# Routing in an attention and mixture-of-experts block: five operations fewer on VectorE, one addition on GpSimd, one more ranks matmul

## The reference

```
x = x + tanh(g_xattn) * xattn(layernorm(x), ctx)       # 16 query heads, 4 key heads, head size 128, rope
x = x + tanh(g_ffn)   * ffn(layernorm(x))
# ffn, for every token
probs = softmax(x @ w_router)                          # 8 experts
top_v, top_i = top_k(probs, 2); top_v = top_v / sum(top_v)
routed = sum over the 2 chosen experts of top_v * down(silu(x @ gate) * (x @ up)) * 2.5
ffn = routed + shared expert
```

## Time and profile before

| | |
|---|---|
| median of three runs | 1221.59 us (1221.35 to 1222.02) |
| the profiled execution: its own time, its span | 1223.99 us, 1222.2 us |
| busy: PE, DVE, ACT, POOL | 1199.6, 1037.9, 903.5, 941.1 us |
| granted TensorE clock, mean | 0.998 |

### The profile page before, as it was taken

The page is one execution under the profiler, slowest core; times in us unless marked ns, Lnnn a source line. Parts: engine busy times, 40 slices in busy tenths (PEclk is TensorE's granted clock), DMA queues, the critical chain, the costliest instruction groups (busy, mean ns, idle before and its releaser), DMA issues.

```text
span 1222.2 us, 31455 instructions
## 1 busy us (share of the span) xinstructions
PE 1199.6 (98%) x8765; PEld 1113.0 (91%) x8766; DVE 1037.9 (85%) x3014; ACT 903.5 (74%) x3774; POOL 941.1 (77%) x1124
## 2 busy tenths in 40 slices
PE   6899999999999999999999999999999999999999
PEld 3788999999999999999999999999999999999887
DVE  8788999999999999999989999988888777777554
ACT  7978787887888778887888877877777646666422
POOL 2778888888888888888888888888888525555585
PEclk9999999999999999999999999999999999999999
DMA  6634233332222222223333333332235636555485
GB/s 178 201 105 127 83 99 104 111 97 90 90 90 90 90 92 93 90 95 94 96 96 114 107 101 99 105 102 80 75 108 151 225 105 192 158 164 159 149 274 183
DMA packets 141079, 148.55 MB, mean 122 GB/s; under 512 B 13824, under 2 KB 124672, under 8 KB 140256
## 3 DMA queue, kind: packets, MB, share of 16 engines
q1 hardware_dynamic: 126096, 125.97, 34.2%
q0 software_dynamic: 6480, 17.77, 4.0%
q10 hardware_dynamic: 8448, 4.20, 1.2%
HBM read 66.93 MB, written 80.76 MB: 121 GB/s over the span
## 4 chain that ended last, share of the span: by engine, by line
PE 92%; DVE 4%; ACT 3%; issue 1%; DMA 0%; SPq 0%; DVEq 0%; ACTq 0%
PE b_kv L1801 14%; PE b_q L1787 14%; PE b_o L1885 13%; PE b_sc L1859 9%; PE b_aT L1874 9%; PE b_pT L1867 5%; PE b_qT L1848 4%; PE b_q L2121 3%; PE b_kv L2121 3%; PE b_kT L1844 2%; PE b_kT L2181 1%; PE b_o L2181 1%; PE b_kv L2181 1%; PE b_q L2181 1%; PE b_aT L2138 1%; PE b_pT L2138 1%
## 5 line engine op out<-in xcount | busy, mean ns | idle before, releaser
L1801 PE MATMUL b_kv<-w_group,kv_in_hi 128*128 128x256 f32 x992 | 204.9, 304 | 0.0
L979 ACT ACTIVATE probs<-b_sc,neg_max 128x128 f32<-128x128 f32 x512 | 180.6, 371 | 2.6 <-DVE neg_max L1343 2.1
L773 POOL TENSOR_TENSOR q_rot<-q_rot,q_sin 128x512 f32<-128x512 f32 x128 | 176.7, 1381 | 7.2 <-DVE q_sin L1333 2.4
L769 POOL TENSOR_TENSOR qk_r<-qk_me,minus_half 128x6 f32<-128x6 f32 x128 | 172.0, 1344 | 10.1
L1801 PEld LDWEIGHTS b_kv<-w_group,kv_in_hi 128*128 128x128 f32 x992 | 161.3, 190 | 7.3 <-issue 0.4
L1787 PE MATMUL b_q<-w_group,kv_in_hi 128*128 128x512 f32 x496 | 164.8, 413 | 0.4 <-DVE q_sin L1333 0.4
L1885 PE MATMUL b_o<-wo_hi,aT_hi 128*128 128x256 f32 x480 | 143.5, 299 | 0.3 <-DVE aT_lo L1357 0.3
L1859 PE MATMUL b_sc<-kT,qT 128*128 128x128 f32 x1024 | 136.3, 276 | 6.2 <-ACT qT L968 4.5
L776 POOL TENSOR_TENSOR q_rot<-q_rot,qk_r 128x512 f32<-128x512 f32 x128 | 133.7, 1044 | 10.0
L1801 PE MATMUL b_kv<-w_group,kv_in_lo 128*128 128x256 f32 x496 | 139.6, 282 | 0.0
L962 ACT ACTIVATE junk<-b_q 128x128 bf16<-128x128 f32 x512 | 134.0, 283 | 0.0
(11 more groups left out here) (332 smaller groups left out, 3977.3 us busy)
## 6 DMA issues: line engine op xcount, KB each, us to landing
xs_scratch<-zeros SPq DMA_DIRECT2D x34, 1032.0 KB, 6.2
s_in<-xs_scratch SPq DMA_DIRECT2D x71, 129.0 KB
yT_scratch<-yT SPq DMA_DIRECT2D x32, 256.0 KB
routed<-ys_scratch SPq DMA_DIRECT2D x32, 256.0 KB, 4.3
w_hi_all<-w_scratch SPq DMA_DIRECT2D x3, 1536.0 KB, 14.4
x_in<-in_x SPq DMA_DIRECT2D x32, 128.0 KB, 2.3
ctx_raw<-in_ctxT SPq DMA_DIRECT2D x32, 128.0 KB, 2.5
trig_scratch<-sincos SPq DMA_DIRECT2D x8, 512.0 KB, 5.9
```

What stands on the lines that cost most here:

```text
L769: nc.gpsimd.tensor_tensor(qk_r[g % 2][:], qk_me[:], minus_half[:, 0:REP + NB], ALU.pow).then_inc(r_ready, 1)
L773: nc.gpsimd.tensor_tensor(q_rot[g % 2][:], q_rot[g % 2][:], q_sin[g % 2][:], ALU.add) \
L979: last = nc.scalar.activation(probs[:, j, :], b_sc[:, j * P:(j + 1) * P], ACT.Exp, bias=neg_max[g % 2][:, j:j + 1], accum_out=row_sum[g % ...
L1801: last = nc.tensor.matmul(b_kv[:, s * 2 * HD:(s + 1) * 2 * HD], kv_in[p][a][:, c, 2 * s:2 * s + 2, :], wkv_of(b, c)[:, g % KVH, :], start= ...
```

## The change

For each tile DVE loses five operations: the two that made the shares from tanh (L1418, L1419), one of two comparisons (both are now one operation over 16 columns), the addition to `seen` and the operation that put expert x STRIDE to the rank. The gate and the constant 2.5 / 2 are multiplied into two small constants once, so y_share is one operation from tanh. The addition to `seen` goes to GpSimd for all tiles but the last two. The expert's first row comes out of PE: a constant tensor `starts` holds STRIDE / 128 x expert, and a third matmul with the matrix of ones adds it 128 times. `lead_tanh` moves from the end of g = 3 to g = 0, behind the squares of keys.

```diff
@@ gpsimd, in a unit
+                    if g == 0 and not first:
+                        need(pool, rk_done, t - 1)
+                        nc.gpsimd.tensor_tensor(seen[:], seen[:], mask[:], ALU.add).then_inc(seen_ready, 1)
@@ scalar, in a unit
+                    if g == 0 and not first:
+                        lead_tanh(t - 2)
                     if not (first and u == 0):
                         queries_out(n, g)
...
-                    if g == 3 and not (end or first and p == 0):
-                        lead_tanh(t - 1)
@@ vector: weights_and_mask
-                nc.vector.tensor_copy(top_f[:], top_i[:, 0:TOPK])
+                nc.vector.tensor_copy(top_f[:], top_i[:, 0:TOPK]).then_inc(pick_ready, 1)
+                need(dve, pick_ready, 2 * t + 1)
+                each = [P, TOPK, E]
+                nc.vector.tensor_tensor(pick[:], expert_no[:].unsqueeze(1).to_broadcast(each),
+                                        top_f[:].unsqueeze(2).to_broadcast(each), ALU.is_equal).then_inc(pick_ready, 1)
                 need(dve, lead_done, t + 1)
-                nc.vector.tensor_scalar(share[:, 0:1], lead_t[:], ROUTED_SCALE / 2, ROUTED_SCALE / 2, ALU.mult, ALU.add)
-                nc.vector.tensor_scalar(share[:, 1:2], lead_t[:], -ROUTED_SCALE / 2, ROUTED_SCALE / 2, ALU.mult,
-                                        ALU.add).then_inc(share_ready, 1)
-                need(dve, share_ready, t + 1)
-                for n in range(TOPK):
-                    last = nc.vector.tensor_scalar(pick[:, n, :], expert_no[:], top_f[:, n:n + 1], None, ALU.is_equal)
-                last.then_inc(pick_ready, 1)
-                nc.vector.tensor_scalar(y_share[p], share[:], gates[:, 1:2], None, ALU.mult)
-                need(dve, pick_ready, t + 1)
+                need(dve, wsin_ready, 8)
+                nc.vector.scalar_tensor_tensor(out=y_share[p], in0=gate_signed[:], scalar=lead_t[:], in1=gate_half[:],
+                                               op0=ALU.mult, op1=ALU.add)
+                need(dve, pick_ready, 2 * t + 2)
+                need(dve, seen_ready, t + 1)
                 nc.vector.tensor_tensor(mask[:], pick[:, 0, :], pick[:, 1, :], ALU.add).then_inc(mask_ready, 1)
@@ vector: rows_of_tokens, read_ranks
-                nc.vector.tensor_reduce(rank[:], ranked[:], AX.X, ALU.add).then_inc(rank_step, 1)
-                need(dve, rank_step, 2 * t + 1)
-                nc.vector.scalar_tensor_tensor(out=row_f[:], in0=top_f[:], scalar=float(STRIDE), in1=rank[:], op0=ALU.mult,
-                                               op1=ALU.add).then_inc(rank_step, 1)
-                need(dve, rank_step, 2 * t + 2)
+                nc.vector.tensor_reduce(row_f[:], ranked[:], AX.X, ALU.add).then_inc(rank_step, 1)
+                need(dve, rank_step, t + 1)
                 nc.vector.tensor_copy(row_i[p][:], row_f[:]).then_inc(row_ready, 1)
...
-                nc.vector.tensor_tensor(seen[:], seen[:], mask[:], ALU.add) \
-                  .then_inc(seen_ready, 1)
+                if isinstance(t, int) and t >= TILES - 2:
+                    nc.vector.tensor_tensor(seen[:], seen[:], mask[:], ALU.add).then_inc(seen_ready, 1)
@@ vector: first pair, u = 4 and u = 5
+                        nc.vector.tensor_scalar(starts[:], expert_no[:], float(STRIDE // P), None, ALU.mult)
...
+                            for to, m, sign in ((gate_signed, 0, 1), (gate_signed, 1, -1), (gate_half, 0, 1), (gate_half, 1, 1)):
+                                nc.vector.tensor_scalar(to[:, m:m + 1], gates[:, 1:2], sign * ROUTED_SCALE / 2, None,
+                                                        ALU.mult).then_inc(wsin_ready, 1)
@@ tensor: ranks
                 nc.tensor.matmul(b_kT[:, D:D + E], below[:], mask[:], start=True, stop=False)
+                nc.tensor.matmul(b_kT[:, D:D + E], ones[:], starts[:], start=False, stop=False)
                 last = nc.tensor.matmul(b_kT[:, D:D + E], ones[:], seen[:], start=False, stop=True)
```

More of the change, by code:

```diff
@@ L249, in flamingo @@
         lead, lead_t = few[:, 0:1], few[:, 1:2]
-        top_f, share, rank, row_f = [few[:, o:o + TOPK] for o in (4, 6, 8, 10)]
+        top_f, gate_signed, gate_half, row_f = [few[:, o:o + TOPK] for o in (4, 6, 8, 10)]
         pick = sb("pick", [P, TOPK, E], F32, late_at)
@@ L263, in flamingo @@
         assert x_res_at[0] <= x_res_end
-        late_at[0] += 128
+        starts = sb("starts", [P, E], BF16, late_at)
+        assert STRIDE % P == 0 and (E - 1) * (STRIDE // P) <= 256
+        late_at[0] += 64
         G_WIDE, D_WIDE = DC * GU // G_TILES, DN * D // D_TILES
@@ L369, in flamingo @@
         (wr_split, y_coarse, y_fine, below_ready, stats2, var2, ve2_done, rstd2_ready, y_normed, yT_done, yT_hi,
-         yT_lo, lg_done, lg_copied, top_found, lead_ready, lead_done, share_ready, pick_ready,
+         yT_lo, lg_done, lg_copied, top_found, lead_ready, lead_done, pick_ready,
          mask_ready, rk_done, rk_read, seen_ready, rank_step, row_ready) = map(sem, (
@@ L373, in flamingo @@
              "y_normed", "yT_done", "yT_hi", "yT_lo", "lg_done", "lg_copied", "top_found", "lead_ready",
-             "lead_done", "share_ready", "pick_ready", "mask_ready", "rk_done", "rk_read",
+             "lead_done", "pick_ready", "mask_ready", "rk_done", "rk_read",
              "seen_ready", "rank_step", "row_ready"))
```

## The result

The changed kernel takes 1224.16 us (median of 20 runs, 1223.55 to 1225.23), the kernel before in the same comparison 1222.05 (20 runs, 1221.35 to 1223.24): ratio 1.0018, 95% interval 1.0012 to 1.0024, 2.1 us slower. Forecast were 1219.2 and a range up to 1221.8. The profiled execution has a span of 1221.9 us at a granted clock of 0.998.

A forecast was written before the change was run, and what follows sets the result against it. PE was taken as the bound, with 92% of the chain. The terms -2.2 - 0.5 - 0.8 + 0.35 + 0.8 = -2.35 took the median 1221.59 to 1219.2 us, range 1217.8 to 1221.8.

The forecast's parts named there:

- What bounds the kernel: PE is 92% of the chain; its lateness, read from distances between starts, is 2.8 us over 27 tiles.
- the choice of the median: The forecast was taken from the runs' median, 1221.59 us, 2.4 below the profiled execution's 1223.99.
- Tanh, -2.2: Moving lead_tanh behind the squares of keys ends the late units g = 0, mostly behind the loop's jump: 2.2 us gained.
- the first rival: Another wait of the unit, or the jump itself, takes the gain, so the 2.2 stays: 1221.4 us, chance 0.17.
- Second pair, -0.5: Around 128 us the squares of keys no longer stand behind the waiting tanh on the chain: 0.5 us gained once.
- Five operations, -0.8: Less DVE work shortens PE's waits in g = 1 (0.4), at 105 us (0.2) and for the slot table (0.2).
- Constants, +0.35: Five small DVE operations making constants in the first pair, 0.07 each, all on the path: 0.35 us lost.
- Third matmul, +0.8: The added ranks matmul stands where PE is not idle: 32 x 0.026 = 0.8 us lost.
- So I take nothing: In g = 0, GpSimd's 1.33 us reciprocal root was taken not to delay DVE's two-input operations: no cost.
- Both are covered: The addition to seen on GpSimd, 0.2 to 0.3 or at most 0.7, fits in 1.07 us to spare before PE.
- The second rival: GpSimd's root (L769) shuts out DVE's y_share and mask in 14 units behind a jump: 9 us, 1228, chance 0.06.

The follow-up runs named there:

- R + C: Kernel before with routing off DVE, addition to seen on GpSimd, third matmul, and cosine table moved to g = 3; tanh not moved: 1222.27 us against 1222.21.
- T + R + C: The changed kernel with GpSimd's cosine table made one unit earlier, in g = 3: 1218.91 us against 1221.96 for the kernel before.
- T: Kernel before with only lead_tanh moved behind the squares of keys of g = 0: 1221.94 us against 1221.96.
- R: The changed kernel with tanh back at the end of ScalarE's g = 3: 1222.59 us against 1222.49 for the kernel before.
- C: Kernel before with only GpSimd's cosine table moved from g = 0 to g = 3: 1221.75 us against 1222.11.

## Why the prediction was wrong

- **What bounds the kernel**: right. PE's distances showed every effect. The profiled execution of before lay 2.4 over its median; its part behind unit 124 took 281.1, and in all twelve other traces 278.9 to 279.6. So the excess was there, and the choice of the median was right.
- **Tanh, -2.2**: right as a mechanism, and in size once nothing else is as late (R + C has a long stage of 784.95, T + R + C of 782.59). Timeline of ACT, kernel after, behind the jump; the squares of keys start 0.27 after heads_T (389.86), not 0.84, tanh with no idle time ahead of queries_out:

```profile
390.13 0.30 ACT L955 ACTIVATE junk<-b_kv 128x128 bf16<-128x128 f32 x1
...
390.63 0.24 ACT L1042 ACTIVATE few<-few 128x1 f32<-128x1 f32 x1
390.72 0.64 ACT L973 ACTIVATE qT<-b_qT 128x512 f32<-128x512 f32 x1
```

  But PE gets it only if nothing else is as late, and the same units had a second lateness behind the first (T alone: 0.0). I listed that as the first rival with 0.17, in g = 0; it sits in g = 1.
- **Second pair, -0.5**: the amount is right (126.20 to 133.96 is 7.76, before 8.27), but tanh alone gives 0.20 of it (T: 8.07); it takes R as well. And 0.45 of it is given back in the two late units behind it.
- **Five operations, -0.8**: PE's wait for the slot table went from 0.36 to 0.16, as forecast, the one for x_n at 105 us from 0.33 to 0.25 (0.2 forecast); the table's place was the rest of it (C takes it away). Mis-sized where it matters: that these operations also start GpSimd's sums earlier was not in the sum at all. With T and C in place R, third matmul included, is worth 1.7 us in the long stage (784.31 against 782.59) and 2.8 by the medians (-3.1 against -0.3), whose intervals are wide enough for either.
- **Constants, +0.35**: 0.1 in the trace after. The wait at 74.3 went from 0.17 to 0.18, and two units there took 0.04 and 0.05 more; in R and in T + R + C one of them took 0.36 more, so the price is not settled. **Third matmul, +0.8**: paid in full as forecast, but 0.020 in a tile, not 0.026: 0.6 in 32 tiles.
- **The step that failed is "So I take nothing"**: the sum has no term for DVE and GpSimd holding each other off. The cosine table, started 0.3 us earlier by tanh's move and the five operations together, ran into DVE's probabilities. That cost 3.9 us in nine units g = 1 of the long stage and 0.45 in the second pair, nearly all of the 4.5 by which the forecast is off (+2.1 for -2.35). "Both are covered" holds as far as it goes: the addition takes 0.20 as I took it, GpSimd is even again at g = 3, and with the addition back on DVE the late units stay. But I had asked there only how late GpSimd may be for PE, and the harm came from its being early, beside another operation of DVE. And the pair from which I judged whether GpSimd keeps DVE out had the root of the scales in it (L769 of before), the one GpSimd operation that doesn't: in the trace after too DVE works beside it undisturbed (27 masks, each with two inputs in SBUF, last 0.15 to 0.17 there, 18 of them from start to end beside the root). The additions and products do, and the earlier trace rows held that pair as well (393.20 with 393.54). The second rival had the right mechanism, GpSimd shuts DVE out, at the wrong operation and place, with 0.06 of the chance, and priced at 9 us for 3.9.

The Trainium skill, SBUF — State Buffer, section Who interferes with whom, lets a DVE operation with two SBUF inputs and a GpSimd operation that reads SBUF exclude each other, and the second waits for the whole of the first. For the table and the probabilities the traces agree: 1.43 = 1.0 + 0.4. For GpSimd's root they do not: the 27 masks beside it last at most 0.17. The section SBUF: two separate sides adds DVE's two-port modes, by which the one-tensor operations at 363.20 would be held off as well; they were.

## What to carry to other kernels

Before moving or shortening work on one of two engines that exclude each other, list for each long operation of the one what the other runs at that moment, and by how little it is first: here it was 0.03 us behind in one kernel and 0.16 ahead in the other, and 0.43 us of PE hung on it each time. Where an engine waits for two inputs, undoing one lateness shows nothing and undoing both shifts all that follows; try the parts of a change alone and together before giving any of them up, since six of the seven combinations here looked worthless or worse and the seventh gains 3 us. If a long operation has no one waiting for it, move it to where its engine idles; here a wait put ahead of it only moved the collision.

## What was not expected of the hardware

- GpSimd's root (128x6 and 128x1, some 1.33 and 0.56 us) does not hold DVE off; its additions and products do: the addition of 1 column (L760) still takes 0.5 when it meets the probabilities.
- The scatter's issue on GpSimd (L797) and DVE's operations in SBUF hold each other off as well: 1.43 for 1.07, and 1.90 for 0.27 with the table behind it.
- At the loop's jump DVE starts kT (L1344) 0.17 us later after heads_T (332.17 for 331.46, against 302.58 for 302.04 in the middle). It fits that the changed kernel loses the race only in tiles without the jump ahead of them. But with the addition back on DVE two tiles behind a jump lose it as well, and no run took the jump away.
